# Second layer of a graph network on one core: one-hots of the segments first, their products last, the other stages one step further ahead

## The reference

```
gathered = vals[:, None] * x[cols]                       # vals = edge_weight, cols = dst
agg = segment_sum(gathered, rows, num_segments=12500)    # rows = src
return einsum('nc,oc->no', agg, W) + b
```

## Time and profile before

| | us |
|---|---|
| three runs | 13427.5, 13432.33, 13446.26 (median 13432.33) |
| the profiled execution | 13418.83 |
| its span, first to last instruction | 13417.0 |
| busy PE, DVE, ACT, POOL | 9496.7, 8452.5, 5206.1, 7119.9 |

### The profile page before, as it was taken

The page is one execution under the profiler, slowest core; times in us unless marked ns, Lnnn a source line. Parts: engine busy times, 40 slices in busy tenths (PEclk is TensorE's granted clock), DMA queues, the critical chain, the costliest instruction groups (busy, mean ns, idle before and its releaser), DMA issues.

```text
span 13417.0 us, 266215 instructions
## 1 busy us (share of the span) xinstructions
PE 9496.7 (71%) x52864; PEld 8632.6 (64%) x52865; DVE 8452.5 (63%) x20544; ACT 5206.1 (39%) x20064; POOL 7119.9 (53%) x7204
## 2 busy tenths in 40 slices
PE   5677777777777767777466667777777777777776
PEld 2566666666666666666355566666666666676765
DVE  6677777777777767777744455555555555555557
ACT  1344444444444444444222233333333333333332
POOL 0666666666666666665355554444444444444430
PEclk7787778877788778777555555555555555555568
DMA  4555555555555555555111123333333333333334
GB/s 140 150 146 149 144 147 146 147 149 148 147 148 148 148 143 147 145 144 137 51 57 57 57 74 91 91 91 91 91 91 91 91 91 91 91 91 92 91 102 127
DMA packets 1647267, 1533.48 MB, mean 114 GB/s; under 512 B 796445, under 2 KB 1367285, under 8 KB 1646165
## 3 DMA queue, kind: packets, MB, share of 16 engines
q1 hardware_dynamic: 1373910, 848.14, 24.8%
q0 software_dynamic: 272384, 677.07, 18.0%
HBM read 1269.42 MB, written 254.87 MB: 114 GB/s over the span
## 4 chain that ended last, share of the span: by engine, by line
PE 30%; issue 25%; DVE 18%; another core or an unknown queue 13%; DVEq 8%; ACT 3%; SPq 1%; POOL 1%; DMA 1%; ACTq 0%; POOLq 0%
PE bank L1000 8%; PE bank L982 6%; PE bank L1011 6%; DVEq L502 4%; PE bank L990 3%; DVE y_all L1463 2%; ACT arena L1085 2%; PE bank L900 2%; DVEq L356 2%; PE bank L919 2%; DVE acc L1596 1%; DVE ohT L1456 1%; DVE feat L1736 1%; PE bank L910 1%
## 5 line engine op out<-in xcount | busy, mean ns | idle before, releaser
L810 POOL DMA_INDIRECT message_scratch<-ohT,idx x3232 | 3177.1, 983 | 3359.8 <-ACT ohT L1185 2133.7
L763 POOL DMA_INDIRECT kv<-kv_scratch,arena x3520 | 3600.4, 1023 | 2409.5 <-issue 1392.9
L1011 PE MATMUL bank<-feat,kve 128*128 128x128 f32 x8640 | 1906.1, 379 | 182.7 <-DVE feat L1736 178.2
L1011 PEld LDWEIGHTS bank<-feat,kve 128*128 128x128 f32 x8640 | 1678.8, 279 | 240.9 <-DVE arena L1744 125.1
L1085 ACT ACTIVATE arena<-arena,weights 128x65 f32<-128x65 f32 x7040 | 1771.1, 337 | 4.8 <-PE bank L919 4.8
L1000 PE MATMUL bank<-acc,oh 128*128 x6464 | 1671.1, 440 | 93.6 <-issue 10.3
L1744 DVE TENSOR_TENSOR arena<-arena,bank 128x128 f32 x2160 | 599.2, 277 | 1699.0 <-PE bank L1011 1293.7
L1000 PEld LDWEIGHTS bank<-acc,oh 128*128 128x128 f32 x6464 | 1437.3, 327 | 303.7 <-issue 303.6
L1092 ACT ACTIVATE featT<-bank 96x512 f32<-96x512 f32 x880 | 519.5, 590 | 2841.9 <-remote 2190.1
L990 PE MATMUL bank<-ident_b,kv 128*128 128x128 bf16 x3232 | 489.6, 306 | 1564.0 <-DVE kv L1704 1443.3
L900 PE MATMUL bank<-We,featT 96*128 96x128 f32 x7040 | 1169.6, 319 | 579.7 <-ACT featT L1092 419.0
(11 more groups left out here) (220 smaller groups left out, 13837.8 us busy)
## 6 DMA issues: line engine op xcount, KB each, us to landing
kve<-message_scratch SPq DMA_DIRECT2D x2160, 129.0 KB
kve<-nodes_scratch SPq DMA_DIRECT2D x880, 256.0 KB
feat<-in_edge_attr_dram SPq DMA_DIRECT2D x880, 96.0 KB
feat<-block_scratch SPq DMA_DIRECT2D x810, 98.0 KB
kv<-kv_scratch,arena POOLq DMA_INDIRECT x3520
arena<-q_scratch SPq DMA_DIRECT2D x880, 64.0 KB
message_scratch<-ohT,idx POOLq DMA_INDIRECT x3232
feat<-in_edge_attr_dram SPq DMA_DIRECT2D x880, 32.0 KB
```

Source lines behind the costliest of these rows:

```text
L763: pool.indirect_dma_start(kv[:, k, g, :], None, kv_d, bass.IndirectOffsetOnAxis(ap=took[:, j, g, 0:1].bitcast(I32), axis=0)).then_inc(s_ga ...
L810: pool.indirect_dma_start(msg_d, bass.IndirectOffsetOnAxis(ap=idx[:, k, g:g + 1], axis=0), sum_ring[:, k % RING1, g, :], None).then_inc(s_ ...
L1011: op = pe.matmul(banks[SEG_BANKS[sg.slot(BR)]][:, 0:P], mt[:, sg.slot(MT), a, 0:C], seg_oh[:, sg.slot(RING1), a, :], start=(a == 0), stop= ...
```

## The change

In the main loop each engine's step is written in another order, and most stages of the first half run one step further ahead. PE: first `row1_stage` (k+3), `rank_stage` (k+7), `sum1_stage` (k+1), then the three products of the segments. ACT: `posw_stage` (k+6) and `rows_out` (k), the three `seg_rel_stage`, then `take1` (k+5) and `off_stage` (k+3). DVE: the three one-hots of the segments, `onehot1_stage`, `count_stage` (k+9), then the other stages with the three additions spread among them, `rel_stage` now for k+4. SP loads `blk_row` 12 steps ahead instead of 10, and a body for turn -2 is put ahead of the loops. No instruction of a step is added or removed, and the waits of each stage are those of before.

```
         def second(eng, body):
+            body(-2, True, False)
             body(-1, True, False)
...
-            ROWS_AHEAD = 10
+            ROWS_AHEAD = 12
...
-            for n in range(STEPS1, STEPS1 + 2):
+            for n in range(STEPS1, STEPS1 + ROWS_AHEAD - UNROLL1):
...
             def body1(i, pairs, segs):                      # PE
                 for k in range(UNROLL1):
+                    if pairs:
+                        at1(i, k, (row1_stage, 3), (rank_stage, 7), (sum1_stage, 1))
                     if segs:
-                        seg(i, k, 0, 1, pairs, agg1_stage)
-                    if pairs:
-                        at1(i, k, (row1_stage, 3), (sum1_stage, 1))
-                    if segs:
-                        seg(i, k, 1, 1, pairs, agg1_stage)
-                    if pairs:
-                        at1(i, k, (rank_stage, 6))
-                    if segs:
-                        seg(i, k, 2, 1, pairs, agg1_stage)
+                        for b in range(SEGMENT):
+                            seg(i, k, b, 1, pairs, agg1_stage)
...
             def body1(i, pairs, segs):                      # ACT
                 for k in range(UNROLL1):
+                    if pairs:
+                        at1(i, k, (posw_stage, 6), (rows_out, 0))
                     if segs:
-                        seg(i, k, 0, 2, pairs, seg_rel_stage)
+                        for b in range(SEGMENT):
+                            seg(i, k, b, 2, pairs, seg_rel_stage)
                     if pairs:
-                        at1(i, k, (posw_stage, 5), (off_stage, 2), (rows_out, 0))
-                    if segs:
-                        seg(i, k, 1, 2, pairs, seg_rel_stage)
-                        seg(i, k, 2, 2, pairs, seg_rel_stage)
-                    if pairs:
-                        at1(i, k, (take1, 4))
+                        at1(i, k, (take1, 5), (off_stage, 3))
...
                     if own:                                 # DVE
                         seg_blocks(i, k)
+                    if segs:
+                        for b in range(SEGMENT):
+                            seg(i, k, b, 1, pairs, seg_onehot)
                     if pairs:
-                        at1(i, k, (carry_stage, 8))
+                        at1(i, k, (onehot1_stage, 2), (carry_stage, 9), (count_stage, 9))
                     if segs:
                         seg(i, k, 0, 0, pairs, seg_add)
-                        seg(i, k, 0, 1, pairs, seg_onehot)
                     if pairs:
-                        at1(i, k, (onehot1_stage, 2))
+                        at1(i, k, (place_stage, 0), (found_stage, 8))
                     if segs:
                         seg(i, k, 1, 0, pairs, seg_add)
-                        seg(i, k, 1, 1, pairs, seg_onehot)
                     if pairs:
-                        at1(i, k, (found_stage, 7), (place_stage, 0), (count_stage, 8))
+                        at1(i, k, (rel_stage, 4), (in_blk_stage, 10))
                     if segs:
                         seg(i, k, 2, 0, pairs, seg_add)
-                        seg(i, k, 2, 1, pairs, seg_onehot)
                     if pairs:
-                        at1(i, k, (rel_stage, 3), (in_blk_stage, 9), (pick_stage, 1))
+                        at1(i, k, (pick_stage, 1))
...
-            in_blk_stage(Step1(0, 0))
             second(dve, body1)
```

## The result

The changed kernel takes 13019.61 us (median of three, 12996.5 to 13030.8) against 13432.33: a ratio of 0.9688, 95% interval 0.9664 to 0.9711, or 413 us less. The forecast was 11,650, 1,370 us too low and outside its range.

A forecast was written before the change was run, and what follows sets the result against it. Chains of waits from engine to engine were taken to bound both stages. 13,418.8 - 280 (steps alone) - 1510 (main loop) + 10 (segments alone) = 11,639, plus 13.5 for the median: 11,650 us, range 11,400 to 12,250.

The forecast's parts named there:

- The rings: Chains of waits between engines, closed within one step; cut by the change, leaving a PE-DVE ring about 5.0 us at most.
- Steps alone, POOL-bound, -280 us: Stage without segments: POOL's four scatters set the step, 6.55 to 5.15 us over 200 steps, -190 to -300 us.
- Main loop, 5.95 us a step, -1510 us: 592 steps from 8.50 to 5.95 us: 5.3 at high clock, 6.6 to 7.0 at low, about equal shares.
- The clock at 0.70 to 0.80: Main loop: PE's granted clock rises from 0.58 to this as its work gets denser, with PE over 85% busy.
- The edge's stand: DVE standing 6.42 us once a turn; likelier than not gone as the loop's start moves; if kept, +270 to +370 us.
- Loads and ACT free: Main loop: segments' loads and ACT's later stages cost nothing, with 2.9 us to spare at 6.6, 1.6 at 5.3.
- Segments alone, +10 us (-10 to +40): Stage with segments only: same work with one-hots ahead of additions, between -10 and +40 us, taken as +10.
- the step that took POOL as a bound of its own: POOL's scatters, 1.26 us apart, taken as a floor of 5.05 us a step plus the odd longer gap.
- the rivals: Fetch gap stays 0.20, clock stays 0.12, high clock throughout 0.08, new ring 0.06, slower 0.04.
- A new ring of the old length: Rival, chance 0.06: a missed dependence keeps the main loop's step, only steps alone gain; 13,150 us.

The follow-up runs named there:

- e5: The changed kernel, no edit, on a chip of the faster kind (kernel before: 12,201 to 12,205 us): 10,631 us, ratio 0.871.
- e6: Kernel before with PE's new order alone, distances as before, on a chip of the faster kind: 12,867 us, ratio 1.054.
- e9: Kernel before with PE's and DVE's new orders, distances and ACT's order as before, on a chip of the slower kind: 14,067 us, ratio 1.049.
- e11: Kernel before with all the new distances and an extra turn, orders as before, on a chip of the slower kind: 12,566 us.
- e3: Kernel before with padding that left no instruction in the program, so the kernel before itself, on a chip of the faster kind: 12,198 us.
- e7: Kernel before with DVE's new order alone, distances as before, on a chip of the faster kind: 11,827 us, ratio 0.969.
- e17: Changed kernel without POOL's second-layer scatters, segments loading one fixed block, on a chip of the slower kind: 11,157 us, ratio 0.832.
- e16: Changed kernel with SP adding to an unused semaphore 16 times a second-layer step, on a chip of the slower kind: 13,184 us, ratio 0.984.
- e8: Kernel before with 8 one-column memsets ahead of DVE's second layer, on a chip of the faster kind: 11,930 us, ratio 0.978.
- e14: Changed kernel without POOL's second-layer scatters, segments loading one fixed block, on a chip of the faster kind: 10,284 us.

## Why the prediction was wrong, step by step

- **The rings are cut: right.** In e5 PE waits for no rel, and for the ranks' release (L1164) 28.5 us in 2000. The prediction counted the orders and the distances together for it. PE's order alone or both orders lengthen the ring through rel (e6, e9), and e11, with the distances alone, has no wait for rel.
- **Steps alone, POOL-bound, -280 us: wrong in size.** 5.15 forecast; 5.52 on the first kind (200 x (6.49 - 5.52) = 194 us), where it is POOL-bound as said, but a scatter without a rest comes every 1.38 us, not 1.26 to 1.29 (most take 0.96 us and 0.30 to the next as in the earlier trace rows, some longer; why isn't shown); 6.40 in the pair (30 us). All kernels with scatters take 6.3 to 6.6 there on the second kind, whatever their order; without them 3.95.
- **Main loop, 5.95 us a step, -1510 us: right on the first kind, wrong in the pair.** 592 x (7.95 - 5.58) = 1,403 us there, 592 x (8.50 - 7.75) = 444 here. The bound is POOL's 5.56 there, and DVE's 5.54 beside it. The prediction took 5.3 for DVE, with half of its load of registers showing; nearly all of it shows.
- **The clock at 0.70 to 0.80: right in the pair** (0.72), higher on the first kind (0.84). It didn't decide the step: PE is busy 70% in the pair, not over 85%, and at 0.84 the step is no shorter than POOL's.
- **The edge's stand goes: right**, and for the reason given; worth 273 us alone in the kernel before on the first kind.
- **Loads and ACT free: right on the first kind.** In the pair ACT stood 707 us ahead of `take1`'s copies (203 before), where its slow register instructions lie.
- **Segments alone, +10 us (-10 to +40): too small.** It is 57 us in the pair and 65 on the first kind (e5 against e3), and e7, with DVE's order alone, has it too (60).
- **What failed** is the step that took POOL as a bound of its own ("POOL is left: its scatters follow each other at 1.26 us", "POOL's 5.05 plus the odd gap") and the other engines' durations as independent of it. So the terms of -1510 and -280 us came to some -440 and -30. In place of 5.95 the main loop's step is 7.75, and without the scatters it is 5.54 on the same kind (e17): on that kind ACT, DVE, SP and PE don't keep their speed while POOL scatters without a rest. By what means the scatters hold them is open. The kernel before had signs that I didn't read: SP's 174 slow register instructions between 7900 and 12500, and 1,174 more in its first layer.
- None of the rivals was this one. "A new ring of the old length" is the nearest by its time (13,150) and wrong as a mechanism. That the forecast's ratio (0.867) is nearly the 0.871 of the first kind is partly luck: the kernel before has steps of 7.95 there, not 8.50, the steps alone gave less than forecast and the clock rose further.

The size of what was missed follows from e5 and e17. The second kind's first layer is some 890 us longer (6557 against 5662 at the first one-hot). 10,631 + 890 = 11,520 would have been the changed kernel's time with a second layer free of stalls, 130 under the forecast. The measured 13,020 is 1,500 above that. The kernel before pays 13,432 - 12,198 - 890 = 340 us on the second kind too. So 1,160 us of the gain went into stalls that the changed order met there and the old one didn't. That it is the lost rest of POOL which brings them is argued from where the slow instructions lie and from e9, and not shown: no kernel was run on the second kind that differs in the rest alone.

**Still open:** what in the second kind of chip makes the stall (POOL's writing, the landing of its transfers or their semaphore updates; e16 shows that updates have a small part); whether it is the chip; whether the recording of the trace has a share in it, as every run here was recorded and up to two thirds of the updates are missing from the traces just where the stalls are; and why the distances alone do better there than the whole change.

## What to carry to other kernels

Where one engine issues transfers without a rest, don't take the other engines' durations from a profile in which it rests: look for their register instructions over 0.5 us first, as a sign that durations may change and not as a measure of the loss (e16). When a stage is moved to the front of its engine's step, move what it waits for one step ahead with it: PE's new order closed a ring through rel (e6, e9), and one step more distance opened it. Look behind a wait for the engine's own load of registers: the profile named PE for a stand that was DVE's load. Time a pair on more than one chip before its gain is believed or dismissed, and look whether a loop's starting place changed, which alone was worth 2.2% here on the first kind.

## What was not expected of the hardware

- The same program takes 12,201 to 12,205 us on three chips and 13,406 to 13,432 on the others; the same change is worth 12.9% on the former and 3.1% on the latter.
- On the latter, register instructions of 35 to 55 ns took mostly 0.69 to 0.72 us on ACT, DVE and SP, in rows whose ends lie 0.71 us or a multiple of it apart, and never on POOL (at most 44 ns in 665 between 7900 and 12500); a release of PE came 10 us late.
- Their traces of kernels with scatters have 99,000 to 137,000 semaphore updates where the others have 262,000 to 274,000, so an absent update in such a trace says nothing, and many releasers are shown as "remote" or "issue".
- Eight instructions ahead of a loop of 312 decide on 5 fetches and 5.9 us of standing a turn (e3 and e8).
- DVE's load of registers takes 0.75 us and shows almost whole in a full step of DVE (e14).
